# A tile's contribution to the recurrent state, computed directly in the orientation of the state

## The reference, cut to what matters

```python
denom = 1.0 + dt * kdamp + dt ** 2 * A
v = (v - dt4 * A * y + dt4 * u_t[..., None] * Bv_t) / denom
y = y + dt4 * v + dt4 * u_t[..., None] * By_t
o = einsum('bhpn,bhn->bhp', y, Cy_t) + einsum('bhpn,bhn->bhp', v, Cv_t)
```

## Time and profile before

| what | value |
|---|---|
| times of three runs | 570.17, 564.38, 566.69 us |
| median | 566.69 us |
| the profiled execution | 568.01 us, of which the span is 566.3 us |
| granted PE clock, mean | 0.904 of full |
| busy: PE, PEld, DVE, ACT, POOL | 436.1, 354.5, 488.0, 263.5, 201.8 us |
| by engine on the chain that ended last | PE 41%, DVE 32%, POOL 12%, issue 8%, ACT 5% |

### The profile page before, as it was taken

The page is one execution under the profiler, slowest core; times in us unless marked ns, Lnnn a source line. Parts: engine busy times, 40 slices in busy tenths (PEclk is TensorE's granted clock), DMA queues, the critical chain, the costliest instruction groups (busy, mean ns, idle before and its releaser), DMA issues.

```text
span 566.3 us, 9333 instructions
## 1 busy us (share of the span) xinstructions
PE 436.1 (77%) x3220; PEld 354.5 (63%) x3220; DVE 488.0 (86%) x1219; ACT 263.5 (47%) x461; POOL 201.8 (36%) x265
## 2 busy tenths in 40 slices
PE   2970019997979928898989937988789956998997
PEld 1850018885856717686757726777675745786886
DVE  5599998989899999989799999898989997788543
ACT  1651224553565624454547632545537542443463
POOL 2000016768510007667530006676640005767100
PEclk9986557999999968998979976999999996998999
DMA  7400000000000010000000000000000000000000
GB/s 223 141 1 0 0 1 2 1 2 1 1 1 1 2 37 2 1 1 1 2 0 0 3 19 1 2 2 1 1 2 0 1 19 2 2 2 1 0 11 11
DMA packets 8433, 7.05 MB, mean 12 GB/s; under 512 B 1593, under 2 KB 7618, under 8 KB 8258
## 3 DMA queue, kind: packets, MB, share of 16 engines
q1 hardware_dynamic: 8386, 6.46, 3.8%
HBM read 5.41 MB, written 1.05 MB: 11 GB/s over the span
## 4 chain that ended last, share of the span: by engine, by line
PE 41%; DVE 32%; POOL 12%; issue 8%; ACT 5%; DMA 0%; SPq 0%; DVEq 0%; POOLq 0%; ACTq 0%
PE HB L523 6%; DVE tp L1158 4%; PE BC L569 4%; POOL vt L1591 4%; DVE hist L1158 3%; PE OO L551 3%; PE RR L551 3%; DVE mm L1273 3%; PE HB L472 3%; PE HB L531 3%; DVE pr L1273 3%; POOL big L1588 3%; PE GV L591 2%; POOL rinv L1607 2%; DVE mm L1311 2%
## 5 line engine op out<-in xcount | busy, mean ns | idle before, releaser
L1588 POOL TENSOR_TENSOR big<-mm 128x256 f32<-128x256 f32 x64 | 50.0, 781 | 289.9 <-DVE mm L1311 289.9
L569 PE MATMUL BC<-xnT,winT 128*128 128x128 f32 x512 | 78.1, 301 | 76.9 <-DVE mm L1311 76.8
L569 PEld LDWEIGHTS BC<-xnT,winT 128*128 128x128 f32 x512 | 69.3, 210 | 83.1 <-DVE mm L1311 79.7
L1591 POOL TENSOR_TENSOR vt<-mm 128x256 f32<-128x256 f32 x64 | 57.9, 904 | 0.0
L854 ACT ACTIVATE pr<-hist 128x512 f32<-128x512 f32 x32 | 34.0, 1113 | 49.8 <-DVE hist L1158 49.8
L523 PE MATMUL HB<-xnT,w 128*128 128x512 f32 x108 | 55.0, 637 | 2.3 <-ACT gtm L939 1.3
L1158 DVE TENSOR_TENSOR tp<-big,hist 128x256 f32<-128x256 f32 x124 | 51.8, 418 | 1.4
L876 ACT ACTIVATE big<-GV 128x256 f32<-128x256 f32 x60 | 23.0, 384 | 63.8 <-PE GV L594 62.3
L591 PE MATMUL GV<-big,vt 128*128 128x128 f32 x256 | 45.0, 302 | 9.3 <-POOL vt L1591 9.3
L1309 DVE TENSOR_TENSOR mm<-BC,pr 128x512 f32<-128x512 f32 x64 | 44.2, 690 | 5.7
L591 PEld LDWEIGHTS GV<-big,vt 128*128 128x128 f32 x256 | 36.9, 208 | 14.9 <-POOL vt L1591 12.0
(11 more groups left out here) (204 smaller groups left out, 1061.0 us busy)
## 6 DMA issues: line engine op xcount, KB each, us to landing
xr<-in_x SPq DMA_DIRECT2D x4, 256.0 KB, 4.8
winT<-in_w_inT SPq DMA_DIRECT2D x1, 1024.0 KB, 6.3
w<-in_rw SPq DMA_DIRECT2D x1, 1024.0 KB
out<-xr SPq DMA_DIRECT2D x3, 256.0 KB, 2.3
taps<-in_dw_wT SPq DMA_DIRECT2D x1, 512.0 KB, 3.6
w<-in_sw SPq DMA_DIRECT2D x2, 128.0 KB
out<-xr SPq DMA_DIRECT2D x2, 128.0 KB, 1.8
winT<-in_w_inT SPq DMA_DIRECT2D x1, 130.0 KB, 2.5
```

Source lines behind the costliest of these rows:

```text
L569: last = pe.matmul(b[:, j * TS:(j + 1) * TS], winT[:, col:col + NS], xt, start=True, stop=True)
L1588: pool.tensor_tensor(wt[q % 8][:], m[:, 0], m[:, 3], ALU.add)
L1591: pool.tensor_tensor(vt[q % 2][:], view(m, 5 * TS, (-3 * TS, 2), (1, TS)), view(m, 3 * TS, (TS, 2), (1, TS)), ALU.subtract).then_inc(wv_do ...
```

## The change

V^T becomes the stationary operand (128 state rows as its columns) and u the one that streams (64 columns), once for each of the two parts of the state and each head: eight matmuls of 128x64 take the place of four of 64x256. Their result has the state rows on the partitions, as `xi` has. The ACT copy to `rts`, the four transposes of `tail_T`, their semaphores and the buffer go. `state_sum` now waits for `r_done`, and its lag falls from 7 to 6, by which it stands at the head of a step, ahead of `pair` and `tile_out`. Line numbers below are those of each kernel's own file.

```diff
-PRODUCTS, COPIES, SUMS, NORMS, NORMS_C, TAIL, TAIL_T, OUT = 1, 2, 0, 2, 4, 4, 6, 7
-MASK, UBAR, GATES, TILE_OUT, STATE_SUM, STATE = 2, 3, 5, 6, 7, 3
+PRODUCTS, COPIES, SUMS, NORMS, NORMS_C, TAIL, OUT = 1, 2, 0, 2, 4, 4, 7
+MASK, UBAR, GATES, TILE_OUT, STATE_SUM, STATE = 2, 3, 5, 6, 6, 3
...
                 if tile < END:
-                    for h in range(NH):
-                        last = pe.matmul(RR[rows(h), (h // 2) * 2 * NS:(h // 2 + 1) * 2 * NS], u[:, head(h)],
-                                         vts[(NH * tile + h) % 8], start=True, stop=True)
+                    for i in range(2):
+                        for h in range(NH):
+                            last = pe.matmul(RR[:, i * DI + h * HD:i * DI + (h + 1) * HD],
+                                             vts[(NH * tile + h) % 8][:, i, :], u[:, head(h)], start=True, stop=True)
                     last.then_inc(r_done, 1)
...
-            def tail_T(tile):
-
-                pe.wait_ge(rts_done, tile + 1)
-                for i in range(2):
-                    for j in range(2):
-                        last = pe.transpose(RR[:, i * DI + j * 128:i * DI + (j + 1) * 128], rts[:, j, i, :], ident[:])
-                last.then_inc(rt_done, 1)
...
-                    for tile in due(g, k, TAIL_T):
-                        tail_T(tile)
...
-            tail_T(END - 1)
...
-            def rts_copy(tile):
-                act.wait_ge(r_done, tile + 1)
-                if tile:
-                    act.wait_ge(rt_done, tile)
-                act.activation(rts[:], RR[:].rearrange("p (j i n) -> p j i n", j=2, i=2), ACT.Copy)\
-                    .then_inc(rts_done, 1)
...
-                    for tile in due(g, k - 1, TAIL):
-                        rts_copy(tile)
...
             def state_sum(tile):
-                dve.wait_ge(rt_done, tile + 1)
+                dve.wait_ge(r_done, tile + 1)
```

## The result

The changed kernel takes 577.94 us (median of 6 runs), the kernel before 567.51 us (6 runs beside it): a ratio of 1.0189, 95% interval 1.016 to 1.0219. It is slower by 10.4 us, twice the forecast of 5.2, and 0.9 us above the top of the range. The profiled execution has a span of 576.3 us at a mean granted clock of 0.892.

A forecast was written before the change was run, and what follows sets the result against it. It took the chain of work ending last as the bound: PE in full stretches, the tail loop in group 3. Group 0 +1.41, groups 1 and 2 +1.72, group 3 +2.04 gave +5.2, 571.9 us; range 566.5 to 577.

The forecast's parts named there:

- the chain of group 3: Loop from tail to tail in group 3, taken to have no slack: three tails +2.79 us, together +2.04.
- I take the low stretch to be as long as before: About the last tail, PE's stretch at 1.2 GHz keeps its length; new records inside could cost up to 1.8 us more.
- The rival in which longer waits of PE bring another fall: Slow records in two tails at the low clock: +3.6 us, 575.5 us in all, chance 0.13.
- The moved sum: DVE's sum zz one step earlier: +0.06 us at tile 2 of groups 0 to 2; free in group 3.
- its own bounds: Upper side of the forecast's range: scaling of u +0.75, low clock +1.8, scatter of runs some 2.5 us.
- The new matmuls, +0.93 a tail: Contribution in each tail: 16 records at 0.112 us, 1.79 us on PE instead of 0.86.
- both rivals about the pitch: Contribution's records: loads hide, 564.0 us, chance 0.08; or load and stream run in series, 583 us, chance 0.06.
- The transposes and the copy, -2.1 in all: PE time saved: 0.43 us twice in group 0, 0.21 and 0.43 in groups 1 and 2; ACT's copy nothing.
- the term for the scaling: POOL's scaling of u in group 3 overlaps DVE's mix less: -0.25 us a tile, -0.75 in all.
- Tile 2's cover: Groups 0 to 2: output matmuls' 1.77 us wait for the state hides 1.60 us of added delay, so cost 0.
- DVE's loop as the bound of group 3: Rival: DVE's list limits group 3, each tail costs 0.32 us, total +4.1, 570.8 us, chance 0.12.

The follow-up runs named there:

- lag 7: Changed kernel with only the lag of the sum put back from 6 to 7: 575.4 us, ratio 1.012.
- the control: Changed kernel with the same six spare matmuls ahead of the second tail of a group instead of the third: 580.9 us, ratio 1.0221.
- the old matmuls: Changed kernel with the four old matmuls back, contribution left unturned, lag 6: 564.0 us; the same with the sum's lag at 7: 566.9 us.
- Light spares: Kernel before with a few unused matmuls at the end of the scan stages: 570.6 us; the same on the changed kernel: 578.5 us.

## Why the prediction was wrong

The direction was right, and so was the chain of group 3: what the change puts on PE lies on it, what it takes away doesn't. The size was wrong by two, and the step that failed is one sentence, "I take the low stretch to be as long as before".

- **The clock, the step that failed.** I priced it at nothing. The rival in which longer waits of PE bring another fall had 0.13 and 3.6 us, as the price of slow records in two tails, and not of the stretch behind one. What happens behind the third tails is a joint effect of the two halves of the edit. The moved sum delays the products by one sum and slows POOL's scaling of u, so PE waits 0.68 and then 1.15 us ahead of the third tail. Behind that wait the granted clock fell to the lower level in two of the first three groups of the profile. The moved sum also shortens DVE's list in the next stretch from 13.7 to 11.6 us, and the new matmuls have taken PE's slack, so now a low clock decides there: 14.0 instead of 11.6 us. In the profile this is 3.5 us. With lag 7 and in the kernel before the clock fell there too (0.88), and the distance stayed at 13.8 and 13.7. Filling the waits, that of group 3 among them, gave back 6.7 us by the medians; in the profiles 5.1 of 8.4 us lie where a wait was filled, and the rest is the clock ahead of the first tails, which no spare touched. The mechanism is shown, and its size is that 5.1 us of one run each. That filling the wait keeps the clock up is shown (16 of 16 against 24 of 44, and the control); the wait alone isn't enough for a fall, since with the old matmuls PE waits as long and the clock stayed full. Why it falls in some groups and not in others isn't known.
- **The sum without the clock.** With the waits filled the loss is 3.6 us, 0.73% [0.47, 0.98], against a forecast of 5.2; against the kernel before with its own waits filled (568.7) it is 2.5. That nearness is of terms that were off in both directions. The range was drawn a little short as well: its own bounds, 571.9 + 0.75 + 1.8 + 2.5, give 577.0 and not 576.
- **The new matmuls, +0.93 a tail.** The pitch was right: 0.112 us a record, so 1.79 for the 16. The load, not the streaming, sets it, as the rows with 128 and 4 streamed columns said, and both rivals about the pitch (0.054 and 0.166) are out. By the rule in the Trainium skill, "TensorE: Matmul & The Clock Gate", section "The mechanism", it would be 0.166; the trace doesn't agree. What the term lacked is the 0.3 us at the two changes of width: a tail costs 1.21 where PE is full and 1.07 behind a wait. On the kernel before the new form costs 9.3 us by itself.
- **The transposes and the copy, -2.1 in all.** Alone they are worth 0 (1.0002), 0.5 by the tails. For groups 1 and 2 I had seen that GV waits for V; in group 0 the same wait was there, and I took PE's full stretch as if each of its instructions counted. A stretch in which PE is busy throughout can still hold waits shorter than the run-out of a record.
- **The moved sum.** I gave it nothing in groups 0 to 2 and -0.75 in group 3, through a faster scaling of u. It is worth 2.9 us with the old matmuls (566.9 to 564.0), and it shows in groups 0 to 2 (tails two to four 26.6 us apart instead of 27.5); in group 3 it costs 0.1 a tail. The sign of the term for the scaling was wrong: 818 to 948 ns. The gain came on the other side of the same overlap, DVE's mix.
- **Tile 2's cover.** I called it the tightest. Its 1.77 us of wait ahead of the output went, as counted, but the two scalings (`du`, `ub`) took 0.8 more than before, and the output starts 14.8 us behind GV of the tail before it instead of 14.4. So 0.4 us came out of cover.
- **DVE's loop as the bound of group 3** (0.12) is out: it would have let 0.32 a tail through, and all of the 1.07 shows, with 0.12 of slower scaling on top.

## What to carry to other kernels

Before costing an fp32 matmul by its streamed columns, look whether the load of the stationary operand is what sets its pitch: making the wide operand stationary turned four matmuls at 0.22 us into eight at 0.22, and 0.3 us more where full width and column halves now meet. Where an edit lengthens a wait of TensorE by even a microsecond, ask what follows it at half the clock and whether TensorE has slack there; a few spare matmuls in the wait test that in one run, with a control where there is no wait. Then look in the traces where the time came back, since part of it can lie where the test did nothing (3.3 of 8.4 us here). And take an edit with two halves apart early: here each half looked harmless or good on one side, and by the medians nearly half of the loss existed only with both (9.3 and -3.5 us apart, 10.4 together).

## What the runs showed of the hardware

- More time at the full clock is worth something only where TensorE is the bound: at 0.88 the third and fourth tails stayed 13.7 us apart in the kernel before and 13.8 with lag 7, at 0.76 they went from 11.6 to 14.0 in the changed one. Light spares took 40 us from the low time and nothing from the total, since the clock was 0.66 again in the 5 us behind them, where TensorE was full; where it was 1.00 there, the first tail came at least 1.3 us earlier.
- In the changed kernel the clock fell behind two of the three third tails with waits of 0.7 and 1.15 us ahead of them, and behind that of group 3. With six spare matmuls in the waits the clock stayed full behind all four third tails, and in the two profiles that is worth 5.1 us.
- A record with 128 weight columns and 64 streamed ones takes 0.112 us at a full clock. Where such records meet records in column halves, about 0.15 us is lost at each change (0.20 and 0.16 instead of 0.10 and 0.11 on the way in, 0.21 and 0.15 instead of 0.11 and 0.10 on the way out).
- An elementwise operation of DVE and one of POOL, both between SBUF tiles, lengthen each other: in the kernel before `xi` takes 0.69 us at its shortest and 1.10 at its longest, `ub` 0.61 and 1.06. Moving a sum of 0.67 us by one step changed both means by 0.12 to 0.13 us, in opposite directions.
